# A spectral attention block on one core: the first stage's normalising and the attention's column weights are dealt out anew among the engines

## What is computed

```python
xn = (x - mean(x, -1)) / sqrt(var(x, -1) + 1e-6)          # first normalisation, over the last axis
tokens = instance_norm(xn)                                 # over a whole image
k, q, v = fno_layer(tokens, ...)                           # 16 heads, made of spectra
attn = softmax(q @ k^T / scale) @ v                        # per batch and head, over 32 tokens
attn = instance_norm(fno_layer(attn, proj ...) + tokens)   # value and projection weights meet here
m = mixer layers with spectra, gelu and instance norms     # 32x17 modes
x = x + (instance_norm(m) + attn)
t = layernorm(x); wx = batchnorm(t @ W^T)
y[s] = sigmoid(wx[s] + y[s-1] @ V^T)                       # recurrence
out = x + y
```

## Time and profile before

| what | us |
|---|---|
| median of 3 runs | 474.27 (474.26 to 479.56) |
| the profiled execution's own time | 473.51 |
| its span | 471.4 |
| busy: TensorE, VectorE, ScalarE, GpSimd | 361.6, 345.7, 263.7, 234.0 |

### The profile page before, as it was taken

The page is one execution under the profiler, slowest core; times in us unless marked ns, Lnnn a source line. Parts: engine busy times, 40 slices in busy tenths (PEclk is TensorE's granted clock), DMA queues, the critical chain, the costliest instruction groups (busy, mean ns, idle before and its releaser), DMA issues.

```text
span 471.4 us, 7104 instructions
## 1 busy us (share of the span) xinstructions
PE 361.6 (77%) x2409; PEld 279.3 (59%) x2409; DVE 345.7 (73%) x946; ACT 263.7 (56%) x530; POOL 234.0 (50%) x276
## 2 busy tenths in 40 slices
PE   0169999998948998899961956867777488999970
PEld 0169986884528998788861843433334135766970
DVE  3698512888969573999948477777778837899992
ACT  0778762620135874556511305989888797899200
POOL 1399960000027957999210567777666985300000
PEclk9979999999997999999995885998898979999995
DMA  8999896789140002999977000000000000000698
GB/s 214 264 295 309 234 296 180 163 233 424 81 179 2 1 1 24 118 129 143 126 93 87 2 0 0 3 0 0 0 1 1 0 0 1 0 3 0 188 287 243
DMA packets 60696, 50.97 MB, mean 108 GB/s; under 512 B 4513, under 2 KB 54097, under 8 KB 59633
## 3 DMA queue, kind: packets, MB, share of 16 engines
q1 hardware_dynamic: 40928, 41.79, 30.4%
q0 software_dynamic: 16512, 8.39, 14.6%
q10 hardware_dynamic: 3216, 0.30, 0.6%
HBM read 30.45 MB, written 16.88 MB: 100 GB/s over the span
## 4 chain that ended last, share of the span: by engine, by line
PE 34%; DVE 29%; POOL 19%; ACT 6%; issue 5%; ACTq 3%; DMA 1%; SPq 0%; POOLq 0%; DVEq 0%
PE PS L644 31%; POOL BIG L583 8%; DVE BIG L1300 4%; DVE SML L1193 4%; DVE BIG L1474 3%; POOL BIG L623 3%; DVE BIG L1548 2%; POOL BIG L618 2%; PE PS L648 2%; DVE SML L1488 2%; POOL BIG L602 2%; ACTq L1000 2%; ACT BIG L1118 2%; ACT SML L390 2%; DMA BIG<-xn_rows 1%
## 5 line engine op out<-in xcount | busy, mean ns | idle before, releaser
L644 PE MATMUL PS<-CST,BIG 128*128 128x128 f32 (+6 forms) x994 | 129.5, 324 | 22.5 <-ACT BIG L1014 9.4
L644 PEld LDWEIGHTS PS<-CST,BIG 128*128 128x128 f32 (+1 forms) x994 | 114.4, 202 | 41.9 <-issue 11.9
L648 PE MATMUL PS<-CST,BIG 128*128 128x128 f32 (+1 forms) x326 | 54.6, 314 | 47.7 <-ACT SML L390 22.8
L648 PEld LDWEIGHTS PS<-CST,BIG 128*128 128x128 f32 (+1 forms) x326 | 43.9, 194 | 71.8 <-issue 52.3
L596 POOL COPY BIG<-BIG 128x512 f32<-128x512 f32 x24 | 30.5, 1328 | 74.4 <-DMA BIG<-xn_rows 71.3
L1193 DVE BATCH_NORM_STATS2 SML<-BIG 128x6 f32<-128x128 f32 x256 | 53.4, 279 | 6.3 <-DMA BIG<-in_x 5.0
L618 POOL TENSOR_TENSOR BIG<-BIG,SML 128x512 f32<-128x512 f32 x32 | 33.2, 1038 | 45.9 <-DVE SML L1213 28.0
L644 PE MATMUL PS<-BIG 128*128 128x128 f32 (+2 forms) x450 | 53.5, 368 | 2.6 <-DVE BIG L1300 2.1
L390 ACT ACTIVATE BIG<-PS 128x512 f32<-128x512 f32 (+3 forms) x59 | 33.2, 572 | 33.5 <-PE PS L644 26.5
L644 PE MATMUL PS<-BIG,SML 128*128 128x256 f32 (+4 forms) x230 | 48.9, 415 | 0.0
L644 PEld LDWEIGHTS PS<-BIG 128*128 128x128 f32 (+2 forms) x450 | 40.6, 168 | 13.1 <-issue 8.2
(11 more groups left out here) (209 smaller groups left out, 516.0 us busy)
## 6 DMA issues: line engine op xcount, KB each, us to landing
xn_rows<-BIG SPq DMA_DIRECT2D x8, 1024.0 KB, 7.7
BIG<-xn_rows SPq DMA_DIRECT2D x8, 1024.0 KB, 9.3
BIG<-in_x POOLq DMA_DIRECT2D x8, 1024.0 KB, 11.0
out_x<-BIG SPq DMA_DIRECT2D x32, 256.0 KB, 3.6
BIG<-wy_rows SPq DMA_DIRECT2D x16, 192.0 KB, 5.4
BIG<-BIG SPq DMA_DIRECT2D x16, 192.0 KB, 4.0
BIG<-in_L_conv_mixer_w SPq DMA_DIRECT2D x2, 544.0 KB, 7.4
CST<-in_const SPq DMA_DIRECT2D x1, 547.5 KB, 8.7
```

Source lines behind the costliest of these rows:

```text
L644: return pe.matmul(o, l, rhs, start=start, stop=stop, **k)
L648: return pe.matmul(o, i, ident[0:n, 0:n], is_transpose=True, start=True, stop=True)
```

## The change

- LN_POOL becomes 8, 8, 5 x 12, 8 (the sum stays 84).
- GpSimd no longer works out the column weights; after the four copies of `qk_c` its first work is the rows.
- ScalarE no longer makes the two scaled copies. Its three copies of transposed weights (`aqk`, `w_t`, `v_t`) move from ahead of the first root to behind the root of chunk 1.
- VectorE makes all of `wy`, behind the coefficients of the last chunk and ahead of its small ops.
- SyncE stores `wy` and issues the 16 broadcasts behind all 8 stores of normalised chunks; WR_AFTER goes.

```diff
-LN_POOL = [4, 8] + 6 * [12]
+LN_POOL = [8, 8, 12, 12, 12, 12, 12, 8]
-WR_AFTER = [0, 0, 0, 0, 5, 10, 13, 16]
@@ sync
                 sp.dma_start(xn_row[:, tokens, :], x_h[:, tokens, :]).then_inc(S(XN_OUT[c]), 16)
-                if c == 2:
-                    sp.wait_ge(S("wy3"), 2)
-                    sp.dma_start(wy_rows, ...).then_inc(S("wy_out"), 16)
-                if c == 4:
-                    sp.wait_ge(S("wy_out"), 16)
-                    sp.wait_ge(S("rs_filled"), 48 // P1_T)
-                    sp.wait_ge(S("xn_0_3"), 64)
-                for n in range(wr_next, WR_AFTER[c]):
-                    sp.dma_start(wr[...], wy_rows[n:n + 1, :].to_broadcast(...)).then_inc(S("rep_w"), 16)
-                wr_next = WR_AFTER[c]
+            sp.wait_ge(S("wy3"), 2)
+            sp.dma_start(wy_rows, ...).then_inc(S("wy_out"), 16)
+            sp.wait_ge(S("wy_out"), 16)
+            sp.wait_ge(S("rs_filled"), 48 // P1_T)
+            sp.wait_ge(S("xn_0_3"), 64)
+            for n in range(NH):
+                sp.dma_start(wr[...], wy_rows[n:n + 1, :].to_broadcast(...)).then_inc(S("rep_w"), 16)
@@ gpsimd
             last.then_inc(S("qk_c"), 1)
-            pool.wait_ge(S("wy_skip"), 1)
...
@@ scalar
-            act.wait_ge(S("w_in"), 16 * 6)
-            for part in range(2):
-                last = act.activation(wy[:, :, 1 + part, :], w_proj[...], ACT.Copy, scale=wcp[:, 1952:1953])
-            last.then_inc(S("wy_skip"), 1)
-            act.wait_ge(S("wt_filled"), 1)
-            act.activation(aqk.rearrange("m k n -> m (k n)"), PS[:, 4, 0:64], ACT.Copy)
-            act.activation(w_t, PS[:, 5, 0:128], ACT.Copy)
-            act.activation(v_t, PS[:, 5, 128:256], ACT.Copy).then_inc(S("wt"), 1)
             root(ln_r[:, 0:XR], row_var[:, 0:XR], "eps_c")
             for c in range(XC):
...
                 if c + 1 < XC:
                     root(...)
+                if c == 0:
+                    act.wait_ge(S("wt_filled"), 1)
+                    act.activation(aqk.rearrange("m k n -> m (k n)"), PS[:, 4, 0:64], ACT.Copy)
+                    act.activation(w_t, PS[:, 5, 0:128], ACT.Copy)
+                    act.activation(v_t, PS[:, 5, 128:256], ACT.Copy).then_inc(S("wt"), 1)
                 if c:
                     spectra(c - 1)
@@ vector, behind the loop over ln_moments and ln_coefs
+            dve.wait_ge(S("w_in"), 16 * 6)
+            for part in range(2):
+                last = TS(wy[:, :, 1 + part, :], w_proj[:, :, 1:1 + MW, part].rearrange("n h w -> n w h"),
+                          wcp[:, 1952:1953], None, ALU.mult)
+            link(last)
+            for part, (p, q, op) in ((0, (0, 0, ALU.add)), (0, (1, 1, ALU.subtract)),
+                                     (1, (0, 1, ALU.add)), (1, (1, 0, ALU.add))):
+                o = lows(wy[:, 0:LW, 1 + part, :])
+                link(TT(wtmp, proj(p), val(q), ALU.mult))
+                link(TT(o, o, wtmp, op))
+            for part in range(2):
+                o = lows(wy[:, 0:LW, 1 + part, :])
+                link(TS(wtmp, val(part), wcp[:, 1953:1954], None, ALU.mult))
+                link(TT(o, o, wtmp, ALU.add))
+            wy_re, wy_im = wy[:, :, 1, :], wy[:, :, 2, :]
+            link(TT(wy[:, :, 0, :], wy_re, wy_im, ALU.add))
+            TS(wy[:, :, 0, :], wy[:, :, 0, :], -1.0, None, ALU.mult).then_inc(S("wy3"), 1)
+            TT(wy_im, wy_im, wy_re, ALU.subtract).then_inc(S("wy3"), 1)
```

More of the change, by code:

```diff
@@ L483, in _ @@
             sp.dma_start(CST[:, n:], t["const"][:, n:]).then_inc(S("const_in"), 16)
-            wr_next = 0
             for c in range(XC):
@@ L489, in _ @@
                 sp.dma_start(xn_row[:, tokens, :], x_h[:, tokens, :]).then_inc(S(XN_OUT[c]), 16)
-                if c == 2:
-                    sp.wait_ge(S("wy3"), 2)
-                    sp.dma_start(wy_rows, wy.rearrange("n w k h -> n (w k h)")).then_inc(S("wy_out"), 16)
-                if c == 4:
-                    sp.wait_ge(S("wy_out"), 16)
-                    sp.wait_ge(S("rs_filled"), 48 // P1_T)
-                    sp.wait_ge(S("xn_0_3"), 64)
-                for n in range(wr_next, WR_AFTER[c]):
-                    sp.dma_start(wr[TB * (n % HG):TB * (n % HG) + TB, n // HG].rearrange("s w k h -> s (w k h)"),
-                                 wy_rows[n:n + 1, :].to_broadcast([TB, 3 * MW * MH])).then_inc(S("rep_w"), 16)
-                wr_next = WR_AFTER[c]
+            sp.wait_ge(S("wy3"), 2)
+            sp.dma_start(wy_rows, wy.rearrange("n w k h -> n (w k h)")).then_inc(S("wy_out"), 16)
+            sp.wait_ge(S("wy_out"), 16)
+            sp.wait_ge(S("rs_filled"), 48 // P1_T)
+            sp.wait_ge(S("xn_0_3"), 64)
+            for n in range(NH):
+                sp.dma_start(wr[TB * (n % HG):TB * (n % HG) + TB, n // HG].rearrange("s w k h -> s (w k h)"),
+                             wy_rows[n:n + 1, :].to_broadcast([TB, 3 * MW * MH])).then_inc(S("rep_w"), 16)
             sp.wait_ge(S("ts"), 3)
@@ L1000, in _ @@
                     act.dma_start(PRM[:, a:a + n], flat(t[name]).to_broadcast([128, n])).then_inc(S("prm"), 16)
-            act.wait_ge(S("w_in"), 16 * 6)
-            for part in range(2):
-                last = act.activation(wy[:, :, 1 + part, :], w_proj[:, :, 1:1 + MW, part].rearrange("n h w -> n w h"),
-                                      ACT.Copy, scale=wcp[:, 1952:1953])
-            last.then_inc(S("wy_skip"), 1)
-            act.wait_ge(S("wt_filled"), 1)
-            act.activation(aqk.rearrange("m k n -> m (k n)"), PS[:, 4, 0:64], ACT.Copy)
-            act.activation(w_t, PS[:, 5, 0:128], ACT.Copy)
-            act.activation(v_t, PS[:, 5, 128:256], ACT.Copy).then_inc(S("wt"), 1)
             root(ln_r[:, 0:XR], row_var[:, 0:XR], "eps_c")
@@ L1228, in _, with lows, val, proj @@
                 ln_coefs(c, "ln_coef")
+            def lows(v):
+                return v.rearrange("n w (q h) -> n w q h", h=8)[:, :, 0::3, :]
+            def val(part):
+                return w_val[:, :, 1:9, part].rearrange("n (k h) w -> n w k h", k=2)
+            def proj(part):
+                return lows(w_proj[:, :, 1:1 + LW, part].rearrange("n h w -> n w h"))
+            dve.wait_ge(S("w_in"), 16 * 6)
[16 more added lines that the diff above has]
+            TT(wy_im, wy_im, wy_re, ALU.subtract).then_inc(S("wy3"), 1)
             dve.wait_ge(S("const_in"), 16)
```

1 line of the change is left out of this document (removed).

## The result

The kernel after takes 472.71 us (median of its runs) beside 475.86 for the kernel before, run on the same chip; the ratio is 0.9923, 95% interval 0.9894 to 0.9952. The ratio leaves out the executions that fell in a slower state of the chip, so it is not quite the quotient of the two medians. So it is faster by 0.8%, about 3.7 us, where I had forecast 7.9. The forecast of 466.4 us was 6.3 too low, and the result lies 1.7 us above the upper end of the range, 471.0. Of these 6.3 us, 1.6 are the kernel before, which now measured 475.86 instead of the 474.27 that I had started from; the rest is the gain, which is less than half of the forecast. The profiled execution took 472.43 us with a span of 470.5.

What follows compares the result with a forecast made beforehand. GpSimd's late rows bounded the first stage; afterwards transfers would be last, at 93.8 us instead of the products' 101.7, gaining 7.9: 474.27 - 7.9 = 466.4 us, range 463.8 to 471.0.

Steps and rivals of the forecast that it cites:

- part 5: SyncE's queue of stores, weights, broadcasts and ts's copies: full, last copy lands at 93.8 us, 7.9 us gained at the products.
- What bounds the kernel now: First stage: GpSimd's normalising rows start late, at 30.2 us, making the stage end at 68.17, with TensorE close behind.
- Part 1: ScalarE's start: products go and copies move, so chunk 0's coefficients are ready at 17.4 us, 3.5 us earlier.
- Part 2: GpSimd's 84 normalising rows: start at 17.4 instead of 30.2, 0.4377 us each, about 2.0 idle, end at 56.2 us.
- Part 3: TensorE's spectra and Gram products become the first stage's bound, ending at 58.5 us, 9.6 us earlier, at full clock.
- Part 4: Column weights on VectorE: 17 operations start at 47.3, take 9.2 us (low 6.2, high 20.7), ready at 56.5.
- The rival in which they come late: VectorE's column weights take 14 us, products come at 96.6, gain is 5.1, total 469.2 us; chance 0.27.
- the slower one: GpSimd's rows hold VectorE's 17 linked weight operations; slower from 19.1 us of work, 475.9 at 20.7 us; chance 0.03.
- The stores: Normalised stores on SyncE's queue: first lands at 40.5 us, each further takes 3.2 at 328 GB/s, eighth lands at 62.9.
- The 32 broadcasts and copies: SyncE's queue behind the stores: 16 broadcasts take 13.2 us, ending at 77.6; ts's 16 copies take 15.2 directly behind.
- The rival "compute sets the end": At the products: broadcasts take 10 us, copies land at 90.6, under compute's 92.1; 9.6 us gained, 464.7 us; chance 0.2.
- No more is gained or lost behind it: From the second batch of products to the end: bound by VectorE's products, transfers move along, the 7.9 us gain stays.

Runs made afterwards that it cites:

- Experiment 7: Changed kernel with 8 broadcasts behind ts's copies, without VectorE's 12 small or its five large column-weight operations; 466.36 and 466.46 us, one run each, results incomplete.
- the second execution: The changed kernel run again without any edit, for a second trace; ratio 0.9923 to the kernel before.
- experiment 8: Changed kernel with 8 broadcasts behind ts's copies, plus four rows of chunk 6 moved from GpSimd to ScalarE; 466.32 us, ratio 0.9789; second series 466.62, 0.9765.
- Experiments 3 and 4: Each against the changed kernel: 8 of 16 broadcasts moved behind ts's copies, 467.64 us, ratio 0.984; weights' store moved to ScalarE's queue, 469.82 us, 0.9884.
- both edits: Changed kernel with 8 broadcasts behind ts's copies and the weights' store on ScalarE's queue, together; 471.73 us, ratio 0.9887.

## Why the prediction was wrong in size, point by point

The step that failed is the end of the transfers in part 5: 93.8 us in the sum, 99.3 in the trace. The mechanism held, and terms of that sum were mis-sized, the stores above all.

- **What bounds the kernel now: right.** GpSimd's late start made the first stage late, and TensorE and the transfers stood close behind.
- **Part 1, first coefficients at 17.4: right** (17.03; the last ones at 46.65 against my 47.3).
- **Part 2, GpSimd's rows: the start right, the end wrong.** I priced all 84 at the 0.4377 of before and got 56.2; the end came at 58.8. I had weighed only how GpSimd holds VectorE (one coefficient operation of 1.22) and not how VectorE's new work holds GpSimd. Experiment 7 assigns about 2.5 us of the loss to it.
- **Part 3, TensorE as the bound, 58.5: wrong by 1.6.** It waited for GpSimd and ended at 60.06 (about 61 in the second execution). With fewer rows on GpSimd it ended at 58.8 (experiment 8). The full clock that I took for this stage was granted (1.00 from 0 to 60 us).
- **Part 4, weights on VectorE: right**, 8.9 us against 9.2, ready at 55.6 against 56.5. The total was a choice between bounds of 6.2 and 20.7, so that it came this close is partly luck. The rival in which they come late is refuted, and so is the slower one, which needed 19.1 us. The Trainium skill, GPSIMD Engine Reference, section 8 (Key points), tells of SBUF interfaces that GpSimd shares with VectorE. Had each such operation been held for a whole row, the sum would have been 14.5, which the trace refutes. What it shows is the other side of the sharing: single GpSimd rows of up to 1.335 us beside VectorE's operations.
- **Part 5, the transfers: this is the step that failed.** It named the right chain, and rightly as the last, but its end was 99.3 instead of 93.8, 5.5 us late (98.5 in the second execution, 4.7 late). Three terms make that up.
  - *The stores:* I took 3.2 us each for the seven behind the first, 22.4 in all, from 328 GB/s between 38 and 46 us. They took 25.7 (landings at 41.4 and 67.1), and the first landed 0.9 later than its 40.5: together 4.2 late. It was not supply: the eighth was issued at 58.9 with the one before it still under way (it landed at 62.0). Nor was the stretch a mix of kinds: the last load of x had landed at 36.2 and the constants at 37.6, and up to 46 only stores were under way. What the number hid is that the rate of stores is not constant: high behind other kinds of transfers (345 again from 68 to 70, behind broadcasts), lower once stores follow stores. Three stretches of before, the third with stores alone again:

```profile
38.00:42.00 4.00, 4.00 (x38) 4.00 (x37) 3.23 (x18) 3.41 (x10) 4.00 (x11) 1.00 1.15 346
42.00:46.00 4.00, 4.00 (x38) 4.00 (x38) 3.86 (x21) 3.73 (x10) 4.00 (x10) 1.00 1.13 310
47.00:50.00 3.00, 3.00 (x30) 3.00 (x29) 2.96 (x17) 2.44 (x6) 3.00 (x8) 1.00 1.02 291
```

  After does the same: 345 GB/s from 38 to 40 and 285 from 44 to 58. At 285 a store takes 3.7 us, and seven take 25.8. Part of the 25.7 is something else, though: the last store landed 5.1 us behind the seventh, while the engines had been all but idle from 65.2 on. In the second execution it landed 3.5 behind the seventh, at 65.9.
  - *The 32 broadcasts and copies:* 28.4 forecast; from the end of the hole at 68.2 to 98.3 they take 30.1, so 1.7 late. I had split the stretch from 52 to 78 with that same 3.2 a store and had got 13.2 for the broadcasts; they landed 0.90 apart (70.1 to 83.6), which makes 14.3 for sixteen. The copies landed 0.87 apart, except for the last, 1.7 behind its neighbour. From 68.1 to 98.3 the engines moved 6.8 MB by the rates of the stretches, and the 32 transfers are 6.3: the loads issued behind them, from 90.75 on, had begun in front of the last copy.
  - *The latencies:* 64.4 - 62.9 = 1.5 from landing to first data against about 1.1 in the trace, 0.4 early.

  Together 4.2 + 1.7 - 0.4 = 5.5. Experiments 3 and 4 confirm the chain from both sides: taking volume from in front of the copies frees the whole wait, and closing the hole frees part of it. Why the stores slow down is open.
- **The rival "compute sets the end": refuted for the change**, yet it describes the split kernel, where 8 broadcasts fewer stand in front of ts's copies and compute is last. Compute alone would have brought the products at 94.8 in the second execution (98.58 - 3.77), not at 92.1, for the reasons under parts 2 and 3. The rival's own price for the broadcasts, 10 us, was further off than the 13.2.
- **"No more is gained or lost behind it": held** within 1 us up to 388 us, in every trace compared above but that of both edits; in the last stage the profiled execution of after lost 1.7 us more, told above.

The price of the error: I took one rate from a stretch of 8 us just behind the loads and used it for a chain of stores three times as long. The trace of before held the slower rate as well, 291 GB/s from 47 to 50 us, which alone makes the seven stores 2.8 us longer. My range had 1 to 2 us for this.

## What to carry to other kernels

When loads move behind all stores of a queue, write the queue out as one chain with a rate for each kind of transfer, and compare its end with the compute chain; here the room was 0.6 us before the change and minus 2.6 after it. Take each rate from several stretches in which only that kind runs, late ones too, and let the range span them. Put in such a queue first what the next step needs and the rest behind it: half the broadcasts moved back doubled the gain of the whole change. Where work moves to an engine beside a busy GpSimd, price what it does to GpSimd's own instructions as well.

## What the runs showed of the hardware that was not expected

- Stores alone moved 345 GB/s just behind the loads (38 to 40 us of after, DMA share 1.14) and 285 later on (44 to 58, share 1.03); broadcasts, and copies within SBUF, 227 and 223, again at a full share. A full share says that the engines are occupied, not how much they move. Why the stores slow down is open.
- GpSimd's row of 128x128, 0.44 us for most of the stage, took up to 1.33 us where VectorE's operations of 16x512 stood beside it, and up to 0.78 with only those of 16x128, though both run on only 16 partitions.
- TensorE's granted clock between 72 and 78.5 us was 0.50 in one execution and 1.00 in the next, with the same code, whose first stage ended at 60.06 and at about 61.
